# Row sums of attention heads on two engines: VectorE takes the second halves of tiles 2 and 3 of four, not of tile 3 alone

## The reference

```python
q = (x @ Wq).reshape(B, S, HEADS, DIM_HEAD)        # 1024 tokens, 8 heads of 64
k = (context @ Wk).reshape(B, L, HEADS, DIM_HEAD)  # 6404 keys
v = (context @ Wv).reshape(B, L, HEADS, DIM_HEAD)
attn = softmax(einsum('bshd,blhd->bhsl', q, k) * DIM_HEAD ** -0.5)
out = einsum('bhsl,blhd->bshd', attn, v) @ Wo + bo
```

## Time and profile before

| what | before |
|---|---|
| median of 3 runs | 1399.79 us (1399.04 to 1400.19) |
| the profiled execution | 1399.33 us, its span 1397.5 us |
| mean granted TensorE clock | 0.978 |
| busy, of the span | PE 96%, DVE 73%, POOL 69%, ACT 58% |

### The profile page before, as it was taken

One profiled execution on the slowest core, in us unless ns is written; L12 is line 12 of the kernel. 1 busy time (PEld: TensorE's weight loads), 2 busy tenths in 40 slices (PEclk: granted clock), 3 DMA queues, 4 the chain that ended last, 5 costly groups with the idle time before them and its releaser, 6 DMA issues.

```text
span 1397.5 us, 19682 instructions
## 1 busy us (share of the span) xinstructions
PE 1348.3 (96%) x6195; PEld 773.9 (55%) x6195; DVE 1013.2 (73%) x1422; ACT 808.5 (58%) x1614; POOL 965.3 (69%) x561
## 2 busy tenths in 40 slices
PE   5989999877999999999999999999999999999998
PEld 3877776523455455545554555554555555555864
DVE  8986665698887677767776776686867666676765
ACT  3458887422566666556655655565666555555731
POOL 5001112342889999999999999999999999998210
PEclk8999999975999999999999999999999999999999
DMA  6640000220000200020020010002001100000200
GB/s 164 203 149 18 17 18 11 51 46 2 1 1 1 51 9 0 19 42 1 1 52 9 1 38 22 1 0 52 8 1 32 24 1 0 9 1 24 87 1 15
DMA packets 77882, 41.38 MB, mean 30 GB/s; under 512 B 63821, under 2 KB 69598, under 8 KB 77510
## 3 DMA queue, kind: packets, MB, share of 16 engines
q1 hardware_dynamic: 77798, 40.28, 11.3%
HBM read 26.53 MB, written 13.74 MB: 29 GB/s over the span
## 4 chain that ended last, share of the span: by engine, by line
PE 88%; DVE 10%; issue 1%; ACT 1%; ACTq 0%; DVEq 0%
PE ps L1540 26%; PE ps L1527 15%; PE ps L1528 14%; PE ps L1487 9%; DVE chunk_max L915 4%; DVE chunk_max L1045 3%; PE ps L1474 3%; PE ps L1732 2%; PE ps L1347 2%; PE ps L1348 2%; PE ps L1349 2%; PE ps L1336 2%; PE ps L1338 2%; PE ps L1337 2%; PE ps L1713 1%; PE ps L1714 1%
## 5 line engine op out<-in xcount | busy, mean ns | idle before, releaser
L607 POOL TENSOR_TENSOR psums<-psums,probs 126x1024 f32<-126x1024 f32 (+1 forms) x392 | 821.0, 2094 | 66.4 <-ACT probs L806 11.6
L1045 DVE TENSOR_REDUCE chunk_max<-ps 128x2 f32<-128x1008 f32 (+1 forms) x416 | 473.2, 1183 | 157.2 <-PE ps L1487 156.8
L806 ACT ACTIVATE probs<-ps 126x512 f32<-126x512 f32 (+1 forms) x816 | 413.2, 623 | 268.3 <-PE ps L1528 257.0
L1540 PE MATMUL ps<-probs,v_mem 126*64 126x512 f32 (+1 forms) x1632 | 389.8, 598 | 0.0
L1527 PE MATMUL ps<-q_heads,ring 128*126 128x512 f32 (+1 forms) x816 | 335.4, 411 | 0.5
L1528 PE MATMUL ps<-q_low,ring 128*126 128x512 f32 (+1 forms) x816 | 322.3, 395 | 0.0
L1540 PEld LDWEIGHTS ps<-probs,v_mem 126*64 126x64 f32 (+1 forms) x1632 | 111.6, 136 | 173.4 <-issue 123.0
L1527 PEld LDWEIGHTS ps<-q_heads,ring 128*126 128x126 f32 (+1 forms) x816 | 152.0, 186 | 81.2 <-issue 44.3
L750 ACT CAST ring<-ps 64x252 fp32r<-64x252 f32 (+1 forms) x356 | 128.3, 360 | 117.3 <-PE ps L1474 114.2
L1108 DVE TENSOR_TENSOR xn<-xn,probs 126x512 f32<-126x512 f32 x126 | 178.8, 1419 | 21.9 <-ACT probs L806 16.4
L1487 PE MATMUL ps<-ring,q_heads 64*128 64x504 f32 (+1 forms) x416 | 164.2, 470 | 13.5 <-DVE chunk_max L1045 10.7
(11 more groups left out here) (230 smaller groups left out, 1364.7 us busy)
## 6 DMA issues: line engine op xcount, KB each, us to landing
v_scratch<-v_stage SPq DMA_DIRECT2D x51, 252.0 KB
v_mem<-v_scratch SPq DMA_DIRECT2D x8, 1606.5 KB
ctx_mem<-in_ctx_t SPq DMA_DIRECT2D x3, 803.2 KB, 9.0
vslot<-in_ctx_rows SPq DMA_DIRECT2D x51, 47.2 KB
xn<-rden_scratch SPq DMA_DIRECT2D x14, 128.0 KB
pair_w<-in_f_pairs SPq DMA_DIRECT2D x1, 1351.0 KB, 10.8
pair_w<-in_f_pairs SPq DMA_DIRECT2D x1, 965.0 KB, 7.7
pair_w<-in_f_pairs SPq DMA_DIRECT2D x1, 579.0 KB, 4.4
```

Source lines behind the costliest of these rows:

```text
L607: pool.tensor_tensor(sums[0:r, 0:width], sums[0:r, 0:width], probs[0:r, n % PROBS, 0:width], ALU.add).then_inc(c_sum, 1)
L806: act.activation(probs[0:r, n % PROBS, cols(half)], ps[0:r, score_bank(t, half), :], ACT.Exp, scale=float(HD) ** -0.5).then_inc(c_exped, 1)
L1045: dve.tensor_reduce(chunk_max[:, h % 2, i:i + 2, c], ps[:, banks[0]:banks[1] + 1, 0:group_tiles(c) * KT], AX, ALU.max).then_inc(c_reduced, 1)
L1540: ins = pe.matmul(ps[half * HD:(half + 1) * HD, B_ACC, :], v_tiles[0:r, h % 2, t, :], probs[0:r, n % PROBS, cols(half)], start=(t == 0), s ...
```

## The change

In heads 0 to 6 `by_vector` now holds for tiles 2 and 3 of each four. With 51 tiles that is 25 tiles of a head (2, 3, 6, 7, ... 46, 47 and 50) in place of 12. VectorE's list for a block has two adds in a row where it had one, and in block 12, behind the key correction, the add of tile 50. The first add of a head, a copy, is that of tile 2. The counts for `c_sumd` follow. Head 7 stays as it is.

```diff
 def by_vector(h, t):
 
-    return h == HEADS - 1 or t % GT == GT - 1
+    return h == HEADS - 1 or t % GT >= GT // 2
 
 
 def vector_done(h, t):
 
-    before = h * (TILES // GT)
-    return before + (max(t, 1) if h == HEADS - 1 else (t + 1) // GT)
+    if h == HEADS - 1:
+        return h * VECTOR_TILES + max(t, 1)
+    return h * VECTOR_TILES + sum(by_vector(h, n) for n in range(t + 1))
 
 
 def vector_adds(h, t):
 
-    before = h * (TILES // GT)
-    return before + (max(t, 1) if h == HEADS - 1 else t // GT + 1)
+    return vector_done(h, t)
+
+
+VECTOR_TILES = sum(by_vector(0, n) for n in range(TILES))
...
             def add_rows(h, t):
                 n, r = TILES * h + t, rows_of(t)
-                first = 1 if h == HEADS - 1 else GT - 1
+                first = 1 if h == HEADS - 1 else GT // 2
...
                     if h < HEADS - 1 and b:
+                        add_rows(h, b * GT - 2)
                         add_rows(h, b * GT - 1)
                     if b == 2 and h:
                         reciprocals(h - 1)
...
                     g = projected_in(h, b)
                     if g is not None:
                         k_lo(g, B_KEYS)
+                    if h < HEADS - 1 and b == GROUPS_H - 1:
+                        add_rows(h, TILES - 1)
                     if h == HEADS - 1:
                         for t in block_tiles(b)[2:]:
                             add_rows(h, t)
```

## The result

| what | before | after |
|---|---|---|
| median | 1399.99 us (1399.04 to 1402.61, 4 runs) | 1504.11 us (1502.60 to 1505.43, 4 runs) |
| ratio, 95% interval | | 1.074 (1.0722 to 1.0759) |
| span of the profiled execution | 1397.5 us | 1502.1 us |
| mean granted TensorE clock | 0.978 | 0.974 |

The change costs 104.1 us. The predicted time was 1503.0. In the kernel after, code lines from the second edit on stand three lower: the maxima are L1048, VectorE's adds L1111, its copy L1116, POOL's adds L610, the exponentials L809. PE's lines behind VectorE's list stand six lower: the scores for the maxima are L1493, the attention's scores L1533 and L1534.

A forecast was written before the change was run, and what follows sets the result against it. PE was taken to set the block's length before, DVE after. Terms 70 + 4 + 2 + 1 + 27, less 1, gave 103 us on 1399.8: 1503, range 1435 to 1526 (the forecast's own 1480 to 1526).

The forecast's parts named there:

- The regular block: Blocks with an add pair in heads 0 to 6: DVE becomes the bound, 10.45 against 9.24, 1.21 us more each.
- 58 regular blocks, with the four below: Blocks in heads 0 to 6 with a pair of adds and maxima before and behind: 1.21 us each, 70 us.
- the twelve of 10.10 before: Blocks already lengthened by a sum or query projection on PE: 0.35 us more each, 4 us.
- six at b = 11: Blocks b = 11 with maxima of 756 columns: 0.3 us more each, 2 us.
- three of head 0: Blocks of head 0 with a fifth maximum: 1 us more in sum beyond the 70.
- the one of head 4: Block of head 4 lengthened by PE's output projection: loses at most 1.2 us less.
- six turns, with the block behind: Head to head at b = 12, DVE already full: a blocked pair and a free third add, 4.5 us each, 27 us.
- A: Blocks where DVE's add starts first: 0.69 and 3.5 us in all, block stays 9.24; about 1464 us; chance 0.20.
- B: Adds cost their mean of 1.39 us, two fit each block, only turns lose 17 us: 1417; chance 0.07.
- C: POOL is the pacemaker, so relieving it makes the kernel faster, by at most 10.8 us: 1389; chance 0.03.
- The clock: PE's clock falling to 1.2 GHz in its new gaps, within the 0.04 chance for worse than thought.
- under 90%: Sign expected in the profile after: PE busy under 90% in the heads, waiting for the maxima.

The follow-up runs named there:

- one input: Changed kernel with VectorE's adds in heads 0 to 6, except each head's copy, replaced by a one-input row reduction of the same tile; 1407.10 us.
- apart: Changed kernel with the second add of each pair moved behind the two maxima that followed it; 1409.63 us.
- pair first: Changed kernel with VectorE given tiles 0 and 1 of each four (tiles 4 to 41), beside POOL's 512-column adds, the others whole to POOL; 1404.74 us.
- Turn clear: Changed kernel with tiles 44 to 50 of heads 0 to 6 left whole to POOL, 20 tiles a head for VectorE; 1483.05 us.
- pool alone: Kernel before with POOL narrowed as in the change but VectorE's adds unchanged, so some halves are left out; 1398.29 us.
- single trimmed: Kernel before with VectorE's single add (tile 3 of four) kept for tiles 4 to 43 only, less some in heads 0 and 4; 1409.08 us.
- vector alone: Changed kernel with POOL's adds as wide as before the change, so some halves are added twice; 1514.03 us.

## Why the prediction was right

**The regular block** was predicted at 10.45 and is 10.45. Its parts: POOL's lead 0.77 (0.78), first add 2.17 (2.2), second 2.66 (2.76 from the first's end to its own; 2.77 measured, 658.57 to 661.34). That the add's kind and not DVE's queue makes the block long is shown by *one input*, that the place of the adds counts and not their number by *apart*, the partner's width by *pair first*; that one of the two engines stands still while the other adds is read from the rows of who began when. The Trainium skill, "SBUF — State Buffer", Who interferes with whom, names the exclusion, and by it a VectorE reduction on trn2, with at most one SBUF input, never meets it: *one input* agrees, 0.69 us in the same place. The price estimated from that page, a full wait and then the add's own time, was 3.08 for the second add; the rows said 2.67, and 2.66 was measured.

**The sum.** From the block lengths of heads 0 to 6, before to after:

| term | predicted | measured |
|---|---|---|
| 58 regular blocks, with the four below | 1.21 each, 70 | the other 54: mostly 1.17 to 1.33, 66.3 in all |
| the twelve of 10.10 before | 0.35 each, 4 | 0.07 at b = 1, 0.36 at b = 5: 2.6 |
| six at b = 11 | 0.3 each, 2 | 0.79 each (9.13 to 9.92): 4.7 |
| three of head 0 | about 1.5 each | 1.60 to 1.66: 4.9 |
| the one of head 4 | up to 1.2 less than regular | 0.36 in place of 1.21 |
| six turns, with the block behind | 4.5 each, 27 | 4.2 each, 25.3 |
| all | 103 | 104.3 |

The regular blocks carry the result, and they came out for the reason given. That the total is within 1 us of the measured cost is luck on top: the term of b = 1 and 5 is 1.4 us too high, that of b = 11 2.7 too low (the pair takes 5.54 us there, at 739.49, not 4.94), and in the turns a loss that the sum had at nothing, PE's clock, stands partly in the place of one that came out smaller.

The turn was the least certain term, and its size came out near for partly another reason. Predicted was a blocked pair and a free third. The timeline of DVE after, head 2 to 3:

```profile
750.83 1.28 DVE L1059 TENSOR_TENSOR q_low<-ps,diag 8x512 fp32r<-8x512 f32 x2 [0.56 <-PE ps L1498]
752.03 3.44 DVE L1111 TENSOR_TENSOR xn<-xn,probs 126x512 f32<-126x512 f32 x2
755.40 2.31 DVE L1048 TENSOR_REDUCE chunk_max<-ps 128x2 f32<-128x1008 f32 x2
...
758.62 0.69 DVE L1111 TENSOR_TENSOR xn<-xn,probs 104x512 f32<-104x512 f32 x1
759.35 1.21 DVE L1048 TENSOR_REDUCE chunk_max<-ps 128x2 f32<-128x1008 f32 x1
```

The third is free (0.69), as said. Of the pair only the second add is blocked: 3.44 us, not the 4.93 of the predicted block. With the third that is 4.13, 3.0 more than the one add of 1.15, and the turn is 3.0 longer (11.06 against 8.03). The other 1.3 are in the block behind (10.89 against 9.63), and there two things meet: the fourth score waits for the maximum behind tile 50's add, and the clock is at the lower level. They can be told apart, since the turns of heads 4 and 5 have the clock at 1.00: there PE waits 0.84 us for that maximum (until 1036.54 and a like time in head 5), and a turn with its next block takes 21.3 us, against 21.7 to 22.1 where the clock fell. So 2.2 of the 25.3 us are the clock's, which the sum had at nothing, and the adds' part is some 23, not 27.

*Turn clear* has no such fall of the clock in the heads and gets 21 us back; its own turns still are 0.6 longer than before (8.62 against 8.0), which was not followed further.

**The rivals.** A (DVE first) did not happen in a regular block: with the lead that a stalled block gives to POOL the pattern holds itself, as argued. It did happen in single places: *apart*'s second add, and in a way the first add of the turn, which was served first although POOL's had begun 0.27 us before it. B's price is near what an add costs beside narrow ones (1.59 in *pair first*), not here: mean 2.31 us over the 175 of heads 0 to 6, as forecast. C was shown wrong by *pool alone*. The clock, named among the ways to be worse, did fall in PE's new gaps, in four turns and not in the regular blocks (1.00), at the small price above.

**What the prediction had wrong without harm.** Of its signs one did not come: PE is busy 853.4 of 915 us from 371 to 1286 in the heads, 93% and not under 90%; DVE is at 863.4, 94%. The upper end of its range does not follow from its terms: 58 blocks at 1.6 and six turns at 6 with the other terms give 1535, not 1526. And two full POOL adds and two halves are 7.4 us by the earlier trace rows and a little for gaps, not 8.4, which makes it the surer that POOL catches up (it is busy 7.82 us of the block after, its waiting for DVE included).

## What to carry to other kernels

Price an elementwise add on VectorE by what GpSimd does at that moment, not by its own columns or its mean: a mean of 1.39 us here hid adds of 0.69 and of 2.7. If work must move between the two, place each VectorE add where GpSimd is idle, just ahead of GpSimd's add, or beside its shortest ones; putting PSUM-only work between two adds is one way to move the second there. Two adds a block cost 104, 10 or 5 us by their place and partner (the last of these without the adds at a head's end, which alone are worth 21). And before relieving an engine, see whether anything waits for it: POOL without an idle gap in 36 us was still worth nothing.

## What the runs showed that was not expected

The order of VectorE and GpSimd is settled by far smaller leads than the prediction's 0.25 us. In *pool alone* POOL begins 0.01 us ahead, by the rows of DVE and POOL, and DVE's add is blocked in full:

```profile
427.83 2.92 DVE L1108 TENSOR_TENSOR xn<-xn,probs 126x512 f32<-126x512 f32 x1
```

```profile
427.82 2.39 POOL L607 TENSOR_TENSOR psums<-psums,probs 126x1024 f32<-126x1024 f32 x1
```

In *single trimmed* DVE begins at 741.84 and POOL at 741.85; now DVE takes 0.69 and POOL 2.92. It holds in all traces of these runs: where POOL began up to 0.6 us ahead, DVE's add was blocked in 1142 of 1157 cases, and where DVE began up to 0.3 us ahead, or together with POOL, it was free in all 269. The 15 exceptions are of one kind, told next. Small as the leads are, the order is the same in every regular block of seven heads and again in a second run.

Behind the row shift something holds POOL off. In the turn after, the first DVE add (752.03, 0.67 us) was not blocked, although POOL's had begun at 751.76. The rows of DVE and POOL:

```profile
751.43 0.67 DVE L1059 TENSOR_TENSOR q_low<-ps,diag 8x512 fp32r<-8x512 f32 x1
752.03 0.67 DVE L1111 TENSOR_TENSOR xn<-xn,probs 126x512 f32<-126x512 f32 x1
```

```profile
751.76 3.16 POOL L610 TENSOR_TENSOR psums<-psums,probs 126x1024 f32<-126x1024 f32 x1
```

This POOL add lasts until 754.92, 3.16 us where a lone one has 2.39: it began while the shift ran, and seems to have stood still until the add behind the shift was done. The same is seen in all six turns of the kernel after and all six of *vector alone* (POOL 3.13 to 3.18 us, DVE's add 0.67), and in three turns of the kernel before. The shift has one input in PSUM and one in SBUF on 8 partitions. That it can hold POOL off, and is itself not held beside POOL's first add, fits these rows. So does another reading: the add behind the shift begins 0.07 us before the shift ends, where one behind a maximum begins 0.03 after it, and may have got its turn early. Neither was tried by itself, and it stays open.
